# Last layer of a four-layer graph network: the features become the stationary operand for three of four quarters

## Chip, cores, metric

One core of a Trainium2 chip runs one program. The metric is the device time of one execution in microseconds (us), the median of several runs. Everything is fp32 except a uint8 copy of the adjacency's pattern.

## The reference, cut to what matters

x has 4096 rows of 128 features, adj is 4096 x 4096. Four layers follow each other, each on h = relu(layernorm(x)) and added to x. The change touches the last one alone:

```
def _L3_gnn_ref(X, H):
    msg = jnp.matmul(H.T, X)
    inv_deg = 1.0 / H.sum(axis=0)
    inv_deg = jnp.where(jnp.isinf(inv_deg), 0.0, inv_deg)
    return msg * inv_deg[:, None]
h = jnp.maximum(_layernorm(x, axis=-1), 0.0)
x = x + _L3_gnn_ref(h, adj)
```

Row i of the result is the sum over j of adj[j, i] * h[j, :], divided by the sum of column i of adj.

## The kernel before

T = 32 tiles of P = 128 rows cover the 4096 rows; the output is made in Q = 4 quarters of S = 8 tiles (QC = 1024 rows). The code numbers the passes over adj by h = 0 to 4 (the second layer has two heads, h = 1 and 2), and layer 3 and layer 4 stand below for the passes h = 3 and h = 4, the last being `_L3_gnn_ref`.

In a quarter q the loop `run(h, q, hooks)` (line 387) goes over the 32 source tiles k. `products` (line 310) then does 8 products, one for each output tile s: the stationary operand is a 128x128 block of the adjacency tile, the moving operand is G[:, ., k, :], 129 columns wide (DW): 128 features and a column of ones, whose product gives the column sum of adj. Results go to acc, three banks of PSUM (NB = 3) with 3, 3 and 2 output tiles of 129 columns. In layer 4 the adjacency tiles come straight from memory: SyncE (`stream`, called by `layer3`, lines 234 and 250) brings 128x1024 tiles, 512 KB each, into DEEP = 8 slots of stream3, which lies over the memory of the mask. A slot is filled again when TensorE has finished with it (semaphore deep_used).

At the end of a quarter ScalarE's `take` (line 681) copies the three banks to U, each as soon as it is summed (acc_summed), and tells acc_taken; TensorE waits for a bank's acc_taken only when it starts that bank anew. VectorE's `post3` (line 1191) makes the divisors out of the 129th column, multiplies and adds X, and ScalarE issues the store (`store`, line 802). The last quarter is done bank by bank (line 1209 on) and stored by SyncE. U is [P, 8 * 129]; flat is a view of its first 1024 columns.

The order on each engine is the order of the code. `hooks` is a table from k to small groups of work put into the stream behind step k. `quarters` (line 214) is a loop of the hardware, so that its body stands once in the program; a quarter with a fixed number stands apart. Beside acc, PSUM holds turn (two banks, used for transposes) and mix, of whose third bank `one` is the first 128 columns. ring has 5 slots of 1024 columns: slot 0 is R, 1 to 3 hold the weighted adjacency tiles E of layers 1 to 3, slot 4 holds small constants.

Around the start of layer 4: SyncE issues its first 8 tiles once all E of layer 3 are made (line 289). VectorE runs the rest of layer 3's last quarter (`post2`, and `feed` with the statistics for the layer norm), and ScalarE writes the last 8 tiles of G, which TensorE waits for at k = 24 of quarter 0 (f_norm).

Of the kernel before, what the change touches and what calls it, by code (L numbers as in the profile page):

```python
# [30 lines left out]
P = 128  # L31
ALU = mybir.AluOpType
# [32 lines left out]
def graph_layers(nc, x, adj, adj_t, diag, alpha, w0_t, bias0, ff0, ff0_t, ff1_t, attn, g1, b1, g2, b2,  # L65
                 w2, w2_t, a2, out, inputs1):
    N, D = x.shape
    T = N // P
# [14 lines left out]
    with ExitStack() as ctx:  # L83
        def sb(name, shape, dt=F32):
            return ctx.enter_context(nc.sbuf_tensor(name, shape, dt))

        def sem(name):
            return ctx.enter_context(nc.semaphore(name))
# [17 lines left out]
        dev = sb("dev", [P, S])  # L106
        scale = sb("scale", [P, S])
        shift = sb("shift", [P, S])
        cols = sb("cols", [P, 32])
        rq = sb("rq", [P, S])  # L110
        inv = sb("inv", [P, S])
        zero = sb("zero", [P, S])
# [23 lines left out]
        hmean = cols[:, 24:25]  # L136
        seen = cols[:, 25:26]
        first_top, fall, vfix, wfix = [cols[:, i:i + 1] for i in range(26, 30)]
        warm = {ACT.Sqrt: cols[:, 30:31], ACT.Exp: cols[:, 31:32]}

        acc = ctx.enter_context(nc.psum_tensor("acc", [P, NB, BANK], F32))
# [50 lines left out]
        own_made = sem("own_made")  # L192
        inv_ready, divided = sem("inv_ready"), sem("divided")
        post_done = sem("post_done")

        n_var, n_dev, n_scale, n_norm = sem("n_var"), sem("n_dev"), sem("n_scale"), sem("n_norm")
        n_turned, n_wide, ff_done, exp_made, half_made = sem("n_turned"), sem("n_wide"), sem("ff_done"), sem("exp_made"), sem("half_made")
# [4 lines left out]
        def fixed(v):  # L202
            return isinstance(v, int)
# [6 lines left out]

        def width(b):
            return min(3, S - 3 * b)

        def quarters(eng, first, last, body, steps=None, per_turn=0):

            with eng.Fori(first, last + 1) as q:
                if steps:
                    steps.enter(q - first if first else q, per_turn)
                body(q)
            if steps:  # L220
                steps.leave(last + 1 - first)

        def wait(eng, signal, count):

            if not fixed(count) or count > 0:
                eng.wait_ge(signal, count)

        @block.sync
        def _(sp):  # L230
            def load_x(t, n, loaded):
                sp.dma_start(X[:, t:t + n, :], x[t * P:(t + n) * P, :].rearrange("(s p) d -> p s d", p=P)).then_inc(loaded, 16)  # L232

            def stream(src, slots, loaded, used, h, q, some=range(T)):

                L = len(loaded)
                for k in some:
                    if k >= L:
                        sp.wait_ge(used, q * (T - 1) + k - L + 1)
                    elif not fixed(q) and k == L - 1:  # L240
                        sp.wait_ge(acc_summed[NB - 1], q + h * Q)
                    elif not fixed(q):
                        sp.wait_ge(used, q * (T - 1) + k - L + 2)
                    sp.dma_start(slots(k % L), span(src[k * P:(k + 1) * P, :], q * QC, QC))\  # L244
                        .then_inc(loaded[k % L], 16)

            def layer0(q, some=range(T)):
                stream(adj_t, lambda s: ring[:, s, :], slot_loaded, slot_used, 0, q, some)

            def layer3(q):  # L250
                stream(adj, lambda s: stream3[:, s, :], deep_loaded, deep_used, 4, q)

            load_x(0, S // 2, x_first)
            load_x(S // 2, S // 2, x_loaded[0])
            sp.dma_start(w0T, w0_t).then_inc(w0_loaded, 16)
            layer0(0, range(2))
            load_x(S, S, x_loaded[1])
            layer0(0, range(2, STREAM))
            load_x(2 * S, S, x_loaded[2])
            load_x(3 * S, S, x_loaded[3])  # L260
            loads = [(bias0_b, bias0.partition_broadcast(P)), (alphac, alpha.partition_broadcast(P)),
                     (w2raw, w2_t), (attnc[:, 0:4], attn), (attnc[:, 4:6], a2), (dsub[:, :], diag),
                     (proj1[:, 0:D], ff0_t[0]), (ff0T1, ff0_t[1])]
            loads += [(ff0raw[h], ff0[h]) for h in range(HEADS)]
            loads += [(c, v.rearrange("(c o) -> c o", o=1)) for c, v in ((g1c, g1), (b1c, b1), (g2c, g2), (b2c, b2))]
            loads += [(ff1T[:, :, :], ff1_t.rearrange("h c o -> c h o"))]
            assert len(loads) == WEIGHTS
            for dst, src in loads:
                sp.dma_start(dst, src).then_inc(weights_loaded, 16)  # L269
            layer0(0, range(STREAM, T))  # L270
            quarters(sp, 1, Q - 1, layer0)

            sp.wait_ge(qv_summed, 1)
            sp.dma_start(proj2[:, 0:D], w2).then_inc(w2_loaded, 16)

            sp.wait_ge(saved, 16 * Q)

            def bring_back(q):  # L280
                if fixed(q):
                    sp.wait_ge(post_done, 2 * Q)
                else:
                    sp.wait_ge(f_turned, q + 3 * Q)
                sp.dma_start(V[:, :, :].rearrange("p s d -> p (s d)"), span(inputs1, q * QC, QC)).then_inc(back, 16)
            bring_back(0)
            quarters(sp, 1, Q - 1, bring_back)

            sp.wait_ge(e_made, 3 * Q * T)
            layer3(0)  # L290
            quarters(sp, 1, Q - 1, layer3)
            for b in range(NB):
                sp.wait_ge(last_made, b + 1)
                some = slice(3 * b, 3 * b + width(b))
                sp.dma_start(out.rearrange("(t p) d -> p t d", p=P)[:, (Q - 1) * S:, :][:, some, :], V[:, some, :])\
                    .then_inc(stored, 16)
            sp.wait_ge(stored, 16 * (Q - 1 + NB))
# [11 lines left out]
        def _(pe):  # L309
            def products(n, k, lhs, g, done, fix):  # L310

                for s in range(S):
                    b = s // 3
                    if fix and k == EARLY and s % 3 == 0:
                        pe.wait_ge(acc_scaled, fix * NB - NB + b + 1)
                    if k == 0 and s % 3 == 0:
                        wait(pe, acc_taken, n * NB - NB + b + 1 if not (fixed(n) and n == 0) else 0)
                    mm = pe.matmul(acc[:, b, (s % 3) * DW:(s % 3) * DW + DW], lhs[:, s * P:(s + 1) * P], g,  # L318
                                   start=(k == 0 and s % 3 == 0), stop=(k == T - 1), skip_group_check=True)
                    if k == T - 1 and (s % 3 == 2 or s == S - 1):  # L320
                        mm.then_inc(acc_summed[b], 1)
                    elif s == S - 1:
                        mm.then_inc(done, 1)
                    elif fix and k == EARLY - 1 and s % 3 == 2:
                        mm.then_inc(acc_paused[b], 1)
# [166 lines left out]
            run(3, Q - 1, {})  # L492

            run(4, 0, {})
            quarters(pe, 1, Q - 1, lambda q: run(4, q, {}))

        @block.scalar
        def _(act):  # L500
# [299 lines left out]

            def store(q):
                take(q + 4 * Q)
                act.wait_ge(post_done, q + 4 * Q + 1)
                act.dma_start(span(out.rearrange("(t p) d -> p t d", p=P), q * S, S), V[:, :, :]).then_inc(stored, 16)
            quarters(act, 0, Q - 2, store)
            take(5 * Q - 1)

        @block.vector  # L810
        def _(dve):
# [180 lines left out]
                return dict(zip(ks, steps))  # L992

            for i in range(2):
                dve.memset(G[:, i, :, D], 1.0)
            st.mark(dve.memset(hmean, 0.0))
# [186 lines left out]
                run(3, q, at([1, 6, 8, 11, 14, 17], post2(q - 1) + feed(4, q - 1 + 4 * Q, q - 1)))  # L1184
            quarters(dve, 1, Q - 2, stage3, st, STAGE3)
            stage3(Q - 1)
            for step in post2(Q - 1) + feed(4, 5 * Q - 1, Q - 1):
                step()

            def post3(q):
                dve.wait_ge(acc_taken, (q + 4 * Q + 1) * NB)
                st.then(dve.tensor_scalar(zero[:, :], Ud, 0.0, None, ALU.is_equal))  # L1193
                st.then(dve.tensor_tensor(inv[:, :], Ud, zero[:, :], ALU.add))
                st.then(dve.reciprocal(inv[:, :], inv[:, :]))
                st.then(dve.tensor_scalar(zero[:, :], zero[:, :], -1.0, 1.0, ALU.mult, ALU.add))
                st.then(dve.tensor_tensor(inv[:, :], inv[:, :], zero[:, :], ALU.mult))
                if not fixed(q):
                    dve.wait_ge(stored, q * 16)
                for s in range(S):  # L1200
                    ins = dve.scalar_tensor_tensor(V[:, s, :], U3[:, s, 0:D], inv[:, s:s + 1], blocks(X, q, 1, s)[:, 0, :],
                                                   ALU.mult, ALU.add)
                ins.then_inc(post_done, 1)
            post3(0)
            quarters(dve, 1, Q - 2, post3, st, 5)

            dve.wait_ge(stored, (Q - 1) * 16)
            for b in range(NB):
                dve.wait_ge(acc_taken, (5 * Q - 1) * NB + b + 1)
                some = slice(3 * b, 3 * b + width(b))  # L1210
                z, i = zero[:, some], inv[:, some]
                st.then(dve.tensor_scalar(z, U3[:, some, D], 0.0, None, ALU.is_equal))  # L1212
# [37 lines left out]
```

## Time and profile before

| | us |
|---|---|
| median of 3 runs | 1274.88 |
| lowest, highest | 1274.65, 1276.23 |
| span of the profiled execution | 1272.8 |
| TensorE products busy in it | 1246.4 (98%) |
| TensorE weight loads busy | 1235.7 (97%) |
| VectorE busy | 754.2 (59%) |
| ScalarE busy | 349.8 (27%) |

The span runs from the first to the last instruction on the core, in one profiled execution; the metric also contains what lies around it, so that the median stands 2.1 us above this span. In the views PE is TensorE's products, PEld its weight loads, DVE VectorE, ACT ScalarE, SPq and ACTq the queues that issue transfers.
### The profile page before, as it was taken

How to read it: one execution, taken by the hardware profiler on the slowest of the kernel's cores; microseconds unless marked ns; L12 is line 12 of the kernel's file. 1: busy time of each engine (PE TensorE's matmuls, PEld its weight loads, DVE VectorE, ACT ScalarE, POOL GpSimd, SP SyncE). 2: the span in 40 equal slices, each digit the busy share in tenths (PEclk: the TensorE clock that was granted, in tenths of full speed). 3: DMA queues.
4: the chain of work that ended last, by engine and by line, in shares of the span. 5: the costliest groups of instructions: out<-in, count | busy, mean ns of one | idle time of the engine just before them, and what ended most of it. 6: DMA issues, size and time to landing. Idle time of an engine off the chain costs nothing.

```text
span 1272.8 us, 26806 instructions
## 1 busy us (share of the span) xinstructions
PE 1246.4 (98%) x10979; PEld 1235.7 (97%) x10979; DVE 754.2 (59%) x1348; ACT 349.8 (27%) x872; POOL 0.7 (0%) x6
## 2 busy tenths in 40 slices
PE   7999999999999999999999999999999999999997
PEld 6999999999999999999999999999999999999997
DVE  4336363659686868687979797878697850000001
ACT  3313121324835353432333233443232120000000
POOL 0000000000000000000000000000000000000000
PEclk9999999999999999999999999999999999999999
DMA  7678787850000000000000000000000058889884
GB/s 221 228 250 265 253 262 257 270 197 2 18 2 18 0 16 0 16 1 18 2 18 0 16 1 18 2 1 1 1 0 1 1 196 317 313 293 309 294 310 148
DMA packets 49037, 144.40 MB, mean 113 GB/s; under 512 B 5696, under 2 KB 15168, under 8 KB 48960
## 3 DMA queue, kind: packets, MB, share of 16 engines
q1 hardware_dynamic: 45264, 139.63, 32.7%
q10 hardware_dynamic: 3696, 3.67, 0.8%
q8 instruction: 57, 0.93, 0.3%
q14 instruction: 20, 0.16, 0.0%
HBM read 139.09 MB, written 4.19 MB: 113 GB/s over the span
## 4 chain that ended last, share of the span: by engine, by line
PE 83%; DMA 7%; DVE 6%; SPq 2%; ACT 1%; issue 1%; DVEq 0%; ACTq 0%
PE acc L318 77%; DMA ring<-in_adj_t 7%; PE mix L352 2%; DVE ring L982 2%; PE turn L333 1%; PE mix L369 1%; DVE mask L1017 1%; PE turn L329 1%; SPq L269 1%; ACT V L511 1%; SPq L232 0%; DVE stats L829 0%; DVE stats L825 0%; SPq L244 0%; DVE mask L1063 0%
## 5 line engine op out<-in xcount | busy, mean ns | idle before, releaser
L318 PE MATMUL acc<-G,ring 128*128 128x129 f32 x8192 | 942.1, 276 | 13.8 <-DVE mask L1017 9.4
L318 PEld LDWEIGHTS acc<-G,ring 128*128 128x128 f32 x8192 | 927.2, 192 | 23.0 <-DVE mask L1017 6.9
L982 DVE SCALAR_TENSOR_TENSOR ring<-ring,score,mask 128x1024 f32<-128x1024 f32 x384 | 483.7, 1281 | 136.4 <-PE acc L318 130.7
L318 PE MATMUL acc<-G,mask 128*128 128x129 f32 x2048 | 229.0, 275 | 0.0
L318 PEld LDWEIGHTS acc<-G,mask 128*128 128x128 f32 x2048 | 228.8, 192 | 0.1
L1017 DVE TENSOR_SCALAR mask<-ring 128x1024 uint8<-128x1024 f32 (+1 forms) x128 | 88.7, 693 | 133.9 <-DMA ring<-in_adj_t 133.4
L687 ACT COPY U<-acc 128x387 f32<-128x387 f32 (+1 forms) x60 | 25.3, 458 | 269.9 <-PE acc L318 268.7
L1193 DVE TENSOR_SCALAR zero<-U 128x8 f32<-128x8 f32 x3 | 0.5, 172 | 153.5 <-ACT U L687 153.5
L523 ACT ACTIVATE dev<-var 128x8 f32<-128x8 f32 x28 | 5.9, 211 | 246.6 <-DVE var L838 246.6
L652 ACT COPY ring<-turn 128x512 f32<-128x512 f32 x14 | 8.2, 586 | 121.7 <-DVE ring L982 114.0
L503 ACT COPY cols<-ident 128x1 f32<-128x1 f32 x44 | 8.6, 196 | 103.3 <-DVE shift L848 41.0
L511 ACT ACTIVATE V<-X,shift,scale 128x128 f32<-128x128 f32 (+1 forms) x92 | 36.8, 484 | 0.0
L533 ACT ACTIVATE U<-turn,cols 128x512 f32<-128x512 f32 x32 | 23.2, 774 | 45.2 <-PE turn L333 45.2
L507 ACT ACT_TABLE_LOAD x26 | 33.4, 1283 | 1.2 <-PEq L1229 0.8
L352 PE MATMUL mix<-ring,U 128*128 128x128 f32 (+2 forms) x256 | 32.5, 282 | 1.2 <-ACT U L535 1.2
L352 PEld LDWEIGHTS mix<-ring,U 128*128 128x128 f32 x256 | 31.2, 198 | 1.4 <-ACT U L535 1.4
L1212 DVE TENSOR_SCALAR zero<-U 128x3 f32<-128x3 f32 (+1 forms) x3 | 0.5, 163 | 52.8 <-ACT U L687 52.8
L511 ACT ACTIVATE V<-U,shift,scale 128x128 f32<-128x128 f32 x64 | 25.6, 484 | 10.2 <-DVE shift L848 10.2
L587 ACT COPY G<-mix 128x384 f32<-128x384 f32 (+3 forms) x36 | 14.8, 461 | 47.6 <-PE mix L352 47.6
L333 PE MATMUL turn<-ident,V 128*128 128x128 f32 x192 | 25.0, 273 | 2.5 <-ACT V L511 2.5
L511 ACT ACTIVATE V<-X,norms 128x128 f32<-128x128 f32 (+1 forms) x64 | 25.6, 489 | 0.1
L333 PEld LDWEIGHTS turn<-ident,V 128*128 128x128 f32 x192 | 21.7, 141 | 2.9 <-issue 1.7
(129 smaller groups left out, 449.4 us busy)
## 6 DMA issues: line engine op xcount, KB each, us to landing
ring<-in_adj_t SPq DMA_DIRECT2D x128, 512.0 KB, 4.6
mask<-in_adj SPq DMA_DIRECT2D x128, 512.0 KB, 4.6
inputs<-V ACTq DMA_DIRECT2D x4, 512.0 KB, 2.6
V<-inputs SPq DMA_DIRECT2D x4, 512.0 KB, 4.0
X<-in_x SPq DMA_DIRECT2D x3, 512.0 KB, 9.5
out_x<-V ACTq DMA_DIRECT2D x3, 512.0 KB, 8.5
X<-in_x SPq DMA_DIRECT2D x2, 256.0 KB, 3.3
out_x<-V SPq DMA_DIRECT2D x2, 192.0 KB, 2.1
```

The costliest lines, as they stand in the source:

```text
L269: sp.dma_start(dst, src).then_inc(weights_loaded, 16)
L318: mm = pe.matmul(acc[:, b, (s % 3) * DW:(s % 3) * DW + DW], lhs[:, s * P:(s + 1) * P], g, start=(k == 0 and s % 3 == 0), stop=(k == T - 1) ...
L329: return pe.transpose(dst, col.broadcast_to([P, P]), ident[:, :])
L333: mm = pe.transpose(turn[:, s * P:(s + 1) * P], V[:, s, :], ident[:, :])
L352: mm = pe.matmul(mix[:, s // 3, (s % 3) * PW:(s % 3) * PW + wide], U[:, s * P:(s + 1) * P], weights, start=True, stop=True, skip_group_che ...
L507: act.activation(warm[func], ident[:, 0:1], func)
L511: ins = act.activation(dst(s), src(s), func, bias=add(s), scale=mul(s))
L533: ins = act.activation(dst, src, ACT.Identity, bias=bias_, scale=scale_)
L587: ins = act.copy(blocks(G[:, h % 2, :, :], q, c, 3 * b)[:, :, 0:D], got[:, :, 0:D])
L687: act.copy(U[:, b * 3 * DW:b * 3 * DW + w], acc[:, b, 0:w]).then_inc(acc_taken, 1)
L982: dve.scalar_tensor_tensor(E[k % EB], R, rank[h][:, k:k + 1], span(mask, q * QC + k * N, QC), ALU.max, ALU.mult).then_inc(e_made, 1)
L1017: dve.tensor_scalar(span(mask, q * QC + k * N, QC), ring[:, k % STREAM, :], 0.0, None, ALU.is_gt).then_inc(mask_made, 1)
```

## The change

Quarters 0 to 2 of layer 4 are computed the other way round. The stationary operand is the 128x128 block of features G[:, 0, k, 0:D], the moving operand the adjacency tile in two halves of 512 columns. Two banks of acc gather the transposed result, features by output rows. So a step of k has 2 products of 512 columns in place of 8 of 129 (`by_features`).

The column sums are no longer a by-product. VectorE adds the tiles (`column_sums`): even k into ring slot 0 or 2, odd k into slot 1 or 3 (by the quarter's parity), the first two as copies, and then the two partial sums, 33 instructions a quarter. TensorE sums what is left over the partitions with 8 products of one moving column of ones (`columns`, line 517 of the new kernel), behind k = 4 of the next quarter. A slot of stream3 is free only when both TensorE (deep_used, wide_summed) and VectorE (col_added) have used it.

At the end of a quarter ScalarE copies the two banks to flat, 512 columns each (wide_taken). TensorE turns them back with 8 transposes behind k = 2 of the next quarter (`turn_back`), and VectorE makes divisors and output from turn and one behind its sums 6 and 7. The last quarter is computed as before, but its first product waits for both copies of quarter 2, and it carries the transposes and column products of quarter 2. Layer 3's post-processing, which VectorE did without anything between, now stands between the sums of quarter 0. The loops over the quarters of layer 4 are written out.

```diff
@@ SyncE
             def layer3(q):
-                stream(adj, lambda s: stream3[:, s, :], deep_loaded, deep_used, 4, q)
+                for k in range(T):
+                    n = q * T + k - DEEP
+                    if n >= 0:
+                        if k % T == DEEP - 1 and q:
+                            sp.wait_ge(wide_summed, 2 * q)
+                        else:
+                            sp.wait_ge(deep_used, n - n // T + 1)
+                        if n < (Q - 1) * T:
+                            sp.wait_ge(col_added, n + n // T + 1)
+                    sp.dma_start(stream3[:, k % DEEP, :], adj[k * P:(k + 1) * P, q * QC:(q + 1) * QC])\
+                        .then_inc(deep_loaded[k % DEEP], 16)
@@ TensorE
-            run(4, 0, {})
-            quarters(pe, 1, Q - 1, lambda q: run(4, q, {}))
+            def columns(q):
+
+                pe.wait_ge(col_added, (q + 1) * (T + 1))
+                wait(pe, post_done, q and 4 * Q + q)
+                for s in range(S):
+                    mm = pe.matmul(one[:, s:s + 1], column_part(q, 0)[:, s * P:(s + 1) * P], ones,
+                                   start=True, stop=True, skip_group_check=True)
+                mm.then_inc(col_summed, 1)
+
+            def turn_back(q):
+
+                pe.wait_ge(wide_taken, 2 * (q + 1))
+                for s in range(S):
+                    mm = pe.transpose(turn[:, s * P:(s + 1) * P], flat[:, s * P:(s + 1) * P], ident[:, :])
+                mm.then_inc(back_turned, 1)
+
+            def by_features(q, hooks):
+
+                for k in range(T):
+                    pe.wait_ge(deep_loaded[k % DEEP], (q * (T // DEEP) + k // DEEP + 1) * 16)
+                    if q == 0 and k % S == 0:
+                        pe.wait_ge(f_norm, 4 * Q + k // S + 1)
+                    for c in range(2):
+                        if k == 0 and q == 0:
+                            pe.wait_ge(acc_taken, (4 * Q - 1) * NB + c + 1)
+                        elif k == 0:
+                            pe.wait_ge(wide_taken, 2 * (q - 1) + c + 1)
+                        mm = pe.matmul(acc[:, c, :], G[:, 0, k, 0:D], stream3[:, k % DEEP, c * BANK:(c + 1) * BANK],
+                                       start=(k == 0), stop=(k == T - 1), skip_group_check=True)
+                        if k == T - 1:
+                            mm.then_inc(wide_summed, 1)
+                        elif c == 1:
+                            mm.then_inc(deep_used, 1)
+                    if k in hooks:
+                        hooks[k]()
+
+            def behind(q):
+                return {2: lambda: turn_back(q), 4: lambda: columns(q)}
+            by_features(0, {})
+            for q in range(1, Q - 1):
+                by_features(q, behind(q - 1))
+            pe.wait_ge(wide_taken, 2 * (Q - 1))
+            run(4, Q - 1, behind(Q - 2))
@@ ScalarE
             def store(q):
-                take(q + 4 * Q)
+                if q:
+                    act.wait_ge(back_turned, q)
+                for c in range(2):
+                    act.wait_ge(wide_summed, 2 * q + c + 1)
+                    act.copy(flat[:, c * BANK:(c + 1) * BANK], acc[:, c, :]).then_inc(wide_taken, 1)
@@ VectorE
-            for step in post2(Q - 1) + feed(4, 5 * Q - 1, Q - 1):
+
+            def column_sums(q, hooks):
+
+                for k in range(T):
+                    dve.wait_ge(deep_loaded[k % DEEP], (q * (T // DEEP) + k // DEEP + 1) * 16)
+                    if q == 0 and k == 0:
+                        dve.wait_ge(e_made, 3 * Q * T)
+                    if q == 0 and k == 1:
+                        dve.wait_ge(acc_summed[NB - 1], 4 * Q)
+                    part, tile = column_part(q, k), stream3[:, k % DEEP, :]
+                    if k < 2:
+                        if q >= 2:
+                            dve.wait_ge(col_summed, q - 1)
+                        dve.tensor_copy(part, tile).then_inc(col_added, 1)
+                    else:
+                        dve.wait_ge(col_added, q * (T + 1) + k - 1)
+                        dve.tensor_tensor(part, part, tile, ALU.add).then_inc(col_added, 1)
+                    if k in hooks:
+                        hooks[k]()
+                dve.wait_ge(col_added, q * (T + 1) + T)
+                dve.tensor_tensor(column_part(q, 0), column_part(q, 0), column_part(q, 1), ALU.add).then_inc(col_added, 1)
...
+            column_sums(0, at([1, 5, 7, 8, 9, 11], post2(Q - 1) + feed(4, 5 * Q - 1, Q - 1)))
+            for q in range(1, Q - 1):
+                column_sums(q, at([6, 7], post3(q - 1)))
+            for step in post3(Q - 2):
                 step()
```

The order of TensorE's instructions in the whole of layer 4, before: quarter 0, then the loop's body (one quarter, stood for once), in rows of like instructions (a product counts once here).

```order
L318 MATMUL acc<-G,mask 128x129 x256
L216 UNCONDITIONAL_BRANCH
L216 ISA
L226 ISA
L318 MATMUL acc<-G,mask 128x129 x3
L226 REGISTER_ALU
L318 MATMUL acc<-G,mask 128x129 x61
```

And in the new kernel, from the end of layer 3 to the end of the program (L335 is the narrow product, L539 the wide one, L525 the transposes, L517 the column products; acc, turn and mix are PSUM, G the features, mask the memory of the streamed tiles):

```order
L335 MATMUL acc<-G,ring 128x129 x256
L539 MATMUL acc<-mask,G 128x512 x70
L525 MATMUL turn<-ident,U 128x128 x8
L539 MATMUL acc<-mask,G 128x512 x4
L517 MATMUL mix<-cols,ring 128x1 x8
L539 MATMUL acc<-mask,G 128x512 x60
L525 MATMUL turn<-ident,U 128x128 x8
L539 MATMUL acc<-mask,G 128x512 x4
L517 MATMUL mix<-cols,ring 128x1 x8
L539 MATMUL acc<-mask,G 128x512 x54
L335 MATMUL acc<-G,mask 128x129 x24
L525 MATMUL turn<-ident,U 128x128 x8
```

Three times 256 narrow products have become 70 + 4 + 60 + 4 + 54 = 192 wide ones, with two of the three pairs of inserted groups between them; the third pair stands in the narrow last quarter.

VectorE at the start of layer 4, before: the last tiles E of layer 3 (L982), its post-processing (L1168 to L1178) and the statistics (L825 on).

```order
L982 SCALAR_TENSOR_TENSOR ring<-ring,score,mask 128x1024 x14
L1168 TENSOR_SCALAR zero<-U 128x8
L1169 TENSOR_TENSOR inv<-U,zero 128x8
L1170 RECIPROCAL inv<-inv 128x8
L1175 TENSOR_TENSOR U<-U,V 128x8x128
L1178 SCALAR_TENSOR_TENSOR X<-U,X 128x1024
L825 BN_STATS stats<-X 128x6 x4
```

The same place in the new kernel: the sums (L1269, the copies L1266) with layer 3's post-processing (L1234 to L1244) and statistics (L890 on) between them.

```order
L1266 COPY ring<-mask 128x1024 x2
L1234 TENSOR_SCALAR zero<-U 128x8
L1235 TENSOR_TENSOR inv<-U,zero 128x8
L1236 RECIPROCAL inv<-inv 128x8
L1269 TENSOR_TENSOR ring<-ring,mask 128x1024 x4
L1241 TENSOR_TENSOR U<-U,V 128x8x128
L1269 TENSOR_TENSOR ring<-ring,mask 128x1024 x2
L1244 SCALAR_TENSOR_TENSOR X<-U,X 128x1024
L1269 TENSOR_TENSOR ring<-ring,mask 128x1024
L890 BN_STATS stats<-X 128x6 x4
L1269 TENSOR_TENSOR ring<-ring,mask 128x1024
L894 BN_STATS stats<-X 128x6 x4
```

So 2 copies and 8 sums of 1024 columns now stand ahead of the second half of the statistics, where before these steps followed each other directly.

## Rows read from the trace of the kernel before

**Rows 1.** The page: busy tenths in 40 slices of the span, and granted clock.

```profile
PE   7999999999999999999999999999999999999997
DVE  4336363659686868687979797878697850000001
PEclk9999999999999999999999999999999999999999
```

**Rows 2.** Chain that ended last, its last links: start, us, what.

```profile
916.33 57.22 PE acc L318 x512
974.42 290.30 PE acc L318 x2598
```

**Rows 3.** Groups of layer 4, 1036.9 to 1265.6 us: busy us, mean ns | idle before.

```profile
L318 PE MATMUL acc<-G,mask 128*128 128x129 f32 x2048 | 229.0, 275 | 0.0
L318 PEld LDWEIGHTS acc<-G,mask 128*128 128x128 f32 x2048 | 228.8, 192 | 0.1
```

**Rows 4.** Busy time by windows: layer 4, and one quarter of layer 3.

```profile
core 0: us, PE busy (x) PEld busy (x) DVE busy (x) ACT busy (x) POOL busy (x), PEclk, DMA share, GB/s
1036.86:1265.82 228.96, 228.96 (x2049) 228.77 (x2048) 15.43 (x64) 13.79 (x41) 0.00 (x0) 1.00 0.84 296
916.33:973.38 57.05, 57.05 (x512) 57.05 (x512) 45.01 (x54) 13.84 (x36) 0.00 (x0) 1.00 0.00 0
```

**Rows 5.** Timeline around 83 us (start us, us, engine): products of two moving columns.

```profile
83.05 0.75 PEld L428 LDWEIGHTS mix<-cols,ring 128*128 128x128 f32 x6
83.16 0.73 PE L428 MATMUL mix<-cols,ring 128*128 128x2 f32 x6
...
83.72 0.64 PEld L318 LDWEIGHTS acc<-G,ring 128*128 128x128 f32 x5
```

**Rows 6.** Timeline of TensorE, 200 and 337 to 347 us: 132 columns, transposes, 128 columns.

```profile
200.40 1.97 PE L352 MATMUL mix<-ring,U 128*128 128x132 f32 x16
202.20 9.10 PE L318 MATMUL acc<-G,ring 128*128 128x129 f32 x80
...
337.52 1.04 PE L333 MATMUL turn<-ident,V 128*128 128x128 f32 x8
338.39 3.74 PE L318 MATMUL acc<-G,ring 128*128 128x129 f32 x32
...
344.63 1.95 PE L352 MATMUL mix<-ring,U 128*128 128x128 f32 x16
346.42 27.21 PE L318 MATMUL acc<-G,ring 128*128 128x129 f32 x240
```

**Rows 7.** Line 652, a copy of 512 columns from PSUM: ns min/median/max.

```profile
L652 ACT COPY ring<-turn x14: 586/586/587, 278.4 to 975.0; 128x512 f32<-128x512 f32 x14
```

**Rows 8.** Timeline 688 to 693 us: transposes, ScalarE's copies, the products behind them.

```profile
687.80 0.93 PE L333 MATMUL turn<-ident,V 128*128 128x128 f32 x7
...
688.82 1.45 ACT L533 ACTIVATE U<-turn,cols 128x512 f32<-128x512 f32 x2 [1.91 <-PE turn L333]
...
690.39 1.86 PEld L369 LDWEIGHTS mix<-ff1T,U 128*128 128x128 f32 x16
690.40 2.05 PE L369 MATMUL mix<-ff1T,U 128*128 128x128 f32 x16
```

**Rows 9.** Line 1175, an addition of 1024 columns on VectorE: ns min/median/max.

```profile
L1175 DVE TENSOR_TENSOR U<-U,V x4: 1218/1219/1226, 872.1 to 1043.0; 128x1024 f32<-128x1024 f32 x4
```

**Rows 10.** Timeline 1043 to 1060 us: scale and the last 8 tiles of G.

```profile
1048.47 0.20 DVE L844 RECIPROCAL scale<-dev 128x8 f32<-128x8 f32 x1 [0.40 <-ACT dev L523]
...
1049.00 3.19 ACT L511 ACTIVATE G<-X,shift,scale 128x128 f32<-128x128 f32 x8
```

**Rows 11.** Tile in_adj: from issue to landing of the 128 loads of layer 4.

```profile
DMA to landing us min/median/max: 3.9/4.6/10.6
```

**Rows 12.** Transfers, 1033 to 1045 us in 40 slices: GB/s.

```profile
GB/s 0 0 0 177 218 328 246 328 382 437 396 410 382 246 287 369 382 382 369 382 341 314 314 423 423 410 396 369 423 396 410 423 437 423 410 396 437 410 410 396
```

**Rows 13.** Timeline 1030 to 1045 us: the start of layer 4.

```profile
1032.95 11.69 SPq L244 DMA_DIRECT2D mask<-in_adj  x12
1035.93 1.44 ACT L687 COPY U<-acc 128x387 f32<-128x387 f32 x3 [24.39 <-PE acc L318]
...
1036.86 8.31 PE L318 MATMUL acc<-G,mask 128*128 128x129 f32 x72
```

**Rows 14.** Timeline 1215 to 1273 us: the last copies, VectorE's last instruction.

```profile
1264.80 1.44 ACT L687 COPY U<-acc 128x387 f32<-128x387 f32 x3 [55.74 <-PE acc L318]
...
1269.98 0.62 DVE L1218 SCALAR_TENSOR_TENSOR V<-U,inv,X 128x128 f32<-128x128 f32 x2
```

## What the change will do to the time: the prediction

> **What bounds the kernel now.** The page first: TensorE is busy in every tenth of the span and at the granted clock of 2.4 GHz, while VectorE has nothing to do in the last fifth [rows 1]. The last entry of the chain of waits is one unbroken run of line 318, from layer 3 to the last product of layer 4 [rows 2]. So in the stretch that is changed nothing but TensorE sets the time, and the groups of that stretch say it again: 229.0 us of products with 0.0 us idle, over 1024 logical products that the chip runs as 2048 instructions, since an fp32 product is two [rows 3]. By the window over layer 4 a step of k (8 products, 16 instructions) takes 228.96 us less 0.17 for the drain of the last one, over 128 steps: 1.7875 us, or **111.7 ns an instruction**.
>
> What are these 111.7 ns? Weight loads are as full as the products, 228.77 us [rows 4]. Six instructions with only 2 moving columns have their weight loads from 83.05 to 83.72, 112 ns each [rows 5]: with 64 times fewer columns the pace is the same. The 128-column products run 16 in 1.79 us, 111.9 ns [rows 6]. So the narrow stream goes by its weight load, one 128-column fp32 load in 111.7 ns. What the columns cost by themselves shows where the load doesn't decide: the transposes, one instruction each, take 0.87 us for 8, 108.8 ns, and at 132 columns 16 instructions take 1.80 us, 112.5 ns [rows 6]. At 2.4 GHz these are 261 and 270 cycles, two cycles for each column and 5 to 6 besides. A narrow one of 129 would then need 258 + 6 cycles, 110 ns, just under its load.
>
> **Wide products, the gain.** A 512-column instruction should take 1024 + 6 cycles, 429.2 ns, and its load of 112 ns hides behind the one before. A step of k becomes 2 products, 4 instructions: 1.717 us instead of 1.7875, 0.0707 less. Three quarters have 96 steps: **-6.8 us**. The bounds: with no fixed part, 1.7067 us and -7.8; with a fixed part that grows with the columns (108.8 / 128 or 112.5 / 132 a column), 435 to 436.4 ns, 1.740 to 1.746 us and -4.6 to -4.0. I take the constant one, since 128 and 132 columns leave the same 5 to 6 cycles.
>
> **Column sums on TensorE, a cost.** Line 517 of the new kernel has 8 one-column products a quarter, 16 instructions. Their price is the weight load, 111.7 ns by the 2-column row [rows 5]: 1.79 us a quarter. A wide product before them hides the first load, and the next wide one waits for its own, so 16 stay. Three times: **+5.4 us**. All three lie in TensorE's stream, behind k = 4 of the next quarter, and nothing hides them.
>
> **Turning back, a cost.** 8 transposes a quarter at 108.8 ns [rows 6], 0.87 us, three times: **+2.6 us**. The rows show each lasting 273 ns, but the next one starts after 109. The Trainium skill, page TensorE: Matmul & The Clock Gate, Part 4, puts a transpose within a kernel at about 275 ns. At 275 ns each, 24 of them would be 6.6 us and the sum 4.0 us higher; I go by the start-to-start time, as the trace has 8 in 0.87 us at 2.4 GHz.
>
> **Hand-overs between quarters, a cost.** Before, a bank is copied out while the other two are still summed, and TensorE never waits. Now there are two banks and each copy moves 512 columns from PSUM, 0.586 us [rows 7]. The trace shows such a hand-over around 688 us: the last transpose ends at 687.80 + 0.93 = 688.73, ScalarE starts at 688.82, 0.09 later, and ends at 688.82 + 1.45 = 690.27, the first weight load starts 0.12 later and the group of 16 lasts 2.05 instead of 1.95 us, since the first load isn't hidden [rows 8]. A wide instruction ends some 0.165 us after the next could start (275 less 110 ns, [rows 3]). So from the point where the next product could start: 0.165 + 0.09 + 0.586 + 0.12 + 0.10 = 1.06 us until a product that needs the copy starts. Into quarters 1 and 2 the other bank's products (0.858 us) lie between: 0.1 to 0.2 us lost, twice; its own copy is then done in time. Into quarter 3 the kernel waits for both copies ahead of the first narrow product: the whole 1.06. Together **+1.3 us** (0.9 to 1.5).
>
> **What is hidden.** VectorE adds each 128x1024 tile once more: 33 instructions a quarter at 1.22 us [rows 9], two of them copies that I bound by the same 1.22 and by half of it, 40 us in a quarter of 55 us. In quarter 0 the last steps of layer 3's post-processing stand between the sums (about 6 us, from line 1168 on): the scale for the last 8 tiles of G then comes at 1038 + 12 sums x 1.22 + 6 = 1059 instead of 1048.5, and ScalarE needs 3.2 us more [rows 10]; TensorE wants them at k = 24, 1036.86 + 24 x 1.717 = 1078. In quarters 1 and 2 VectorE stops behind sum 6 until TensorE has done k = 4 and the column products, about 11.3 us in. Queued behind that wait are the sums 7 to 31, and on them SyncE's loads (its queue now waits for the sum too) from k = 15 on. TensorE wants that tile at 1.717 x 15 + 2.7 = 28.4 us; the slot's sum is done by about 16, and a tile lands about 5 us after its issue [rows 11]: over 7 us to spare. **Transfers:** a 512 KB tile every 1.717 us is 305 GB/s; the queue moved 437 GB/s in its best slices while it filled [rows 12], against 296 over the layer [rows 4]. Layer 4 starts on the landing of tile 0, as now [rows 11, 13]; tile 2 may be late by hundredths. The steps of the last tiles and the stores are as before, so what follows the last product stays at 7 us [rows 14].
>
> **Sum.** -6.8 + 5.4 + 2.6 + 1.3 = +2.5 us. The profiled execution has a span of 1272.8 us, 2.1 below the median of 1274.88 us; its span would be 1275.3, and the time **1277.4 us**, 0.2% more. A measurement of this kernel tells about 0.2%, 2.55 us, from no change, so the forecast lies at that bound, a hair inside.
>
> **Rivals.**
> - The fixed part grows with the columns (a 512-column stream is held up in itself, as by reads of the moving tile while DMA writes and VectorE reads the same memory). It decides as soon as an instruction takes over 430 ns: slower. Price 2.2 to 2.8 us: 1279.6 to 1280.2. For it: no row has more than 132 columns. Against: with VectorE busy for 45.01 of 57.05 us beside it, TensorE kept 57.22 us for 512, the same 111.8 ns [rows 2, 4]. Chance 0.13.
> - VectorE becomes the bound. A sum then takes over 1.717 us a tile, since it reads a tile that TensorE streams. Each 0.1 us above that costs 9.6 us over 96 tiles. Against: adds of this size took 1.22 us. Chance 0.05, 1281 to 1290.
> - The column products' weight loads hide behind the wide ones altogether. The cost of 5.4 us falls to near nothing: 1272.0. Against: six loads in a row came at 112 ns each though the products between them had 2 columns [rows 5]. Chance 0.02, faster.
> - Wide products overlap each other. The same page of the Trainium skill, section Back-to-back issue gap, has a sustained 81 ns at 128 columns and 131 ns at 512. As a mechanism of this kernel: were an instruction of 512 columns under 223 ns (twice a narrow one), a step would be under 0.9 us, tiles at 437 GB/s (1.20 us) and sums at 1.22 us would set the pace, 96 x (1.7875 - 1.22) = 54 us would go and 9.3 be added: about 1230. Against: four more columns cost 3.7 ns, all of their two cycles each [rows 6]. Chance 0.01.
>
> **Chances.** The forecast's case has 0.75, with its own range of 1276.1 (no fixed part, cheap hand-overs) to 1278.0; it is cut by the bound into 0.40 same and 0.35 slower. With 0.04 left for what I don't see, split between same and slower: faster 0.03, same 0.42, slower 0.55. The range takes in the first rival and the scatter of the runs, 1275.7 to 1280.5.
>
> **What the new profile would show.** Wide instructions 429 ns apart, so 55 us for a quarter of 128 of them (a step over 1.73 us: the first rival). Between them, 16 instructions of one column in 1.8 us and 8 transposes in 0.87. TensorE idle only at the ends of quarters, 1.0 us in front of the narrow last quarter, released by ScalarE's copy. No wait of TensorE for DMA or for VectorE past the first tiles; VectorE busy some 70% of quarters 0 to 2. A last quarter of 57.2 us and 2.7 for its two inserted groups. I am wrong if TensorE waits inside a quarter, or if the wide step isn't within 0.01 us of 1.717.

## The result, and the profile after

The changed kernel takes 1277.64 us (median of 17 runs, 1273.97 to 1280.51), the kernel before 1274.65 (17 runs, 1271.46 to 1276.5): a ratio of 1.0024, 95% interval 1.0016 to 1.0033. It is slower by a quarter of a per cent, where 0.20% was forecast. The profiled execution has a span of 1277.4 us against 1272.8, 4.6 more, and the first reading is where these 4.6 us lie. The windows of the two profiles, changed kernel first, then before (us, busy us of each engine with instructions, clock, transfers' share, GB/s):

```profile
0.10:285.51 285.41, 267.70 (x2269) 261.28 (x2269) 140.60 (x386) 71.64 (x194) 0.70 (x6) 0.99 0.77 246
285.51:1038.75 753.24, 749.73 (x6665) 745.99 (x6663) 593.85 (x880) 263.53 (x638) 0.00 (x0) 1.00 0.02 8
1038.86:1270.37 231.51, 230.83 (x970) 137.83 (x968) 129.09 (x163) 13.45 (x38) 0.00 (x0) 1.00 0.84 293
```

```profile
0.10:283.44 283.34, 267.61 (x2268) 260.98 (x2269) 140.39 (x385) 71.57 (x194) 0.70 (x6) 0.99 0.77 248
283.44:1036.68 753.24, 749.62 (x6664) 745.91 (x6663) 594.02 (x880) 263.88 (x638) 0.00 (x0) 1.00 0.02 8
```

Layer 0 is 2.1 us longer though nothing in it changed; the passes of layers 1 to 3 are equal to 0.01 us in these two profiles; layer 4 went from 228.96 [rows 4] to 231.51 us, **+2.55**, and what follows it is 7.0 us in both. In layer 0 the work waits for transfers: VectorE's masks wait for them, and TensorE waited 12.4 us for the masks, against 9.4 in the profile before. In the ten profiles of this case, all with the same code for layer 0, it ended anywhere from 281.1 to 288.8 us, and layers 1 to 3 took from 753.15 to 753.74 us. So single executions differ by microseconds in layer 0 and by half of one in layers 1 to 3, and the change is read in layer 4, where stretches of the same instructions repeat to 0.1 us.

A part of layer 0's scatter is TensorE's clock. The same stretch of layer 0, changed kernel first, then before:

```profile
101.50:104.90 3.40, 3.08 (x14) 3.08 (x15) 3.27 (x8) 0.00 (x0) 0.00 (x0) 0.50 0.40 155
101.50:104.90 3.40, 3.35 (x28) 3.00 (x27) 3.21 (x8) 0.00 (x0) 0.00 (x0) 1.00 0.77 257
```

Behind an idle time of 2.38 us the granted clock was 1.2 GHz for these 3.4 us, and 14 instructions came where 28 did before, some 1.5 us of work at 111.7 ns each. Of the ten profiles three have such a stretch near 105 us, and their layer 0 is the longest (285.5, 287.2 and 288.8 us; the others end by 284.9).

The page of the changed kernel, in 40 slices (the rows that answer to [rows 1]; PEld is weight loads):

```profile
PE   7998999999999999999999999999999999999997
PEld 6998999999999999999999999999999974444497
DVE  4445363659686868687979797878687878677401
PEclk9999999999999999999999999999999999999999
```

TensorE is as full as before, at the same clock, but in the wide quarters its weight loads are busy for four tenths only, and VectorE is busy for 86%, 71% and 64% of quarters 0, 1 and 2. The weight loads were relieved and TensorE's own stream was not: its timeline in layer 4 (start us, us, engine, line, out<-in) has every term of the sum.

```profile
1038.86 60.49 PE L539 MATMUL acc<-mask,G 128*128 128x512 f32 x140
1099.18 1.04 PE L525 MATMUL turn<-ident,U 128*128 128x128 f32 x8
1100.06 3.60 PE L539 MATMUL acc<-mask,G 128*128 128x512 f32 x8
1103.49 1.84 PE L517 MATMUL mix<-cols,ring 128*128 128x1 f32 x16
1105.19 51.95 PE L539 MATMUL acc<-mask,G 128*128 128x512 f32 x120
1156.98 1.04 PE L525 MATMUL turn<-ident,U 128*128 128x128 f32 x8
1157.86 3.60 PE L539 MATMUL acc<-mask,G 128*128 128x512 f32 x8
1161.29 1.84 PE L517 MATMUL mix<-cols,ring 128*128 128x1 f32 x16
1162.99 46.60 PE L539 MATMUL acc<-mask,G 128*128 128x512 f32 x108
1210.26 5.63 PE L335 MATMUL acc<-G,mask 128*128 128x129 f32 x48 [0.67 <-ACT U L865]
```

Take differences of starts: 8 wide instructions from 1100.06 to 1103.49, 3.43 us, 429 ns each; 8 transposes in 0.88; 16 column instructions in 1.70, and the wide one behind them begins its columns 0.08 late, as its weight load came last, so 1.78 in all. Into quarter 3 there is an idle time of 0.67 us that ScalarE's copy ended. The 140 in the first row have the hand-over into quarter 1 among them: 60.32 us less 140 x 0.4292 leaves 0.23, which is 0.04 at the layer's start and 0.2 at the hand-over.

What TensorE waited for in layer 4, beside its own stream (us in total, times, longest): its products once, its weight loads for ScalarE's copies and for tiles that hadn't landed.

```profile
PE acc L335 <- ACT U L865: 0.7, 1, 0.7
PEld acc L335 <- ACT U L865: 1.5, 1, 1.5
PEld acc L539 <- ACT U L865: 0.9, 2, 0.4
PEld acc L539 <- DMA mask<-in_adj: 0.5, 2, 0.2
PEld acc L539 <- ACT U L745: 0.2, 1, 0.2
```

### The profile page after: what moved, and what is told of

It reads as the page before. It is cut to its first block, busy times and chain, and to the rows that moved or that the text cites. A ratio compares the mean times of both kernels' runs of the same rounds, so it can differ in the third digit from the quotient of the medians.

```text
span 1277.4 us, 24572 instructions
## 1 busy us (share of the span) xinstructions
PE 1248.4 (98%) x9899; PEld 1145.2 (90%) x9899; DVE 868.0 (68%) x1448; ACT 349.1 (27%) x869; POOL 0.7 (0%) x6
## 4 chain that ended last, share of the span: by engine, by line
PE 83%; DMA 7%; DVE 6%; SPq 2%; ACT 1%; issue 1%; DVEq 0%; ACTq 0%
PE acc L335 64%; PE acc L539 13%; DMA ring<-in_adj_t 7%; PE mix L369 2%; DVE ring L1047 2%; PE turn L350 2%; PE mix L386 1%; DVE mask L1083 1%; SPq L285 1%; PE turn L346 1%; SPq L238 1%; ACT V L569 0%; PE mix L517 0%; DVE stats L894 0%; DVE stats L890 0%
## 5 line engine op out<-in xcount | busy, mean ns | idle before, releaser
L335 PE MATMUL acc<-G,ring 128*128 128x129 f32 x8192 | 943.0, 276 | 16.2 <-DVE mask L1083 12.4
L335 PEld LDWEIGHTS acc<-G,ring 128*128 128x128 f32 x8192 | 928.5, 192 | 25.2 <-DVE mask L1083 8.4
L539 PE MATMUL acc<-mask,G 128*128 128x512 f32 x384 | 166.2, 593 | 0.0
L539 PEld LDWEIGHTS acc<-mask,G 128*128 128x128 f32 x384 | 72.5, 190 | 90.0 <-issue 88.3
L1269 DVE TENSOR_TENSOR ring<-ring,mask 128x1024 f32<-128x1024 f32 x90 | 107.3, 1222 | 22.4 <-DMA mask<-in_adj 21.5
L335 PEld LDWEIGHTS acc<-G,mask 128*128 128x128 f32 x512 | 57.4, 192 | 1.5 <-ACT U L865 1.5
L335 PE MATMUL acc<-G,mask 128*128 128x129 f32 x512 | 57.9, 275 | 0.7 <-ACT U L865 0.7
L745 ACT COPY U<-acc 128x387 f32<-128x387 f32 (+1 forms) x51 | 21.5, 459 | 120.5 <-PE acc L335 119.2
L865 ACT COPY U<-acc 128x512 f32<-128x512 f32 x6 | 3.5, 585 | 144.4 <-PE acc L539 144.4
```

Source lines behind the costliest of these rows:

```text
L539: mm = pe.matmul(acc[:, c, :], G[:, 0, k, 0:D], stream3[:, k % DEEP, c * BANK:(c + 1) * BANK], start=(k == 0), stop=(k == T - 1), skip_gro ...
L745: act.copy(U[:, b * 3 * DW:b * 3 * DW + w], acc[:, b, 0:w]).then_inc(acc_taken, 1)
L1269: dve.tensor_tensor(part, part, tile, ALU.add).then_inc(col_added, 1)
```

## Experiments

All were read in layer 4, from the start of TensorE's first instruction of the layer to that of its last: 228.7 us before, 231.2 in the changed kernel. Experiments 1 to 6 are one execution each, and their whole times are not used, since layer 0 is in them: experiment 4 took 1281.17 us with a layer 4 no longer than the changed kernel's.

**1. Is the narrow stream set by its weight loads?**

```diff
-                    mm = pe.matmul(acc[:, b, (s % 3) * DW:(s % 3) * DW + DW], lhs[:, s * P:(s + 1) * P], g,
+                    mm = pe.matmul(acc[:, b, (s % 3) * DW:(s % 3) * DW + w], lhs[:, s * P:(s + 1) * P], g[:, 0:w],
```

with w = 64 in layer 4 of the kernel before, 129 elsewhere.

> The kernel before, with 64 moving columns in place of 129 in every product of layer 4 (half of the features and the column sums are left out of the last layer). Theory, the narrow stream goes by its weight load: layer 4 takes 228.7 us between its first and last product, as before, 111.7 ns an instruction. Rival, the columns decide: an instruction takes 56 ns and the layer goes by its transfers, 150 us or so, the whole some 75 us less.

Measured 228.6 us. The window over layer 4 (columns as above):

```profile
1037.06:1265.92 228.86, 228.86 (x2050) 228.72 (x2048) 15.43 (x64) 13.84 (x41) 0.00 (x0) 1.00 0.85 297
```

Half the columns, the same 111.7 ns an instruction. The columns don't decide, with half of them to spare: in the narrow form 65 of 129 columns are free, and so was the 129th with its column sum. For the load, and against a fixed pace of any instruction, speak the transposes, which follow each other after 109 ns: their loads are shorter. From the changed kernel's layer 4:

```profile
L335 PEld LDWEIGHTS acc<-G,mask 128*128 128x128 f32 x512 | 57.4, 192 | 1.5 <-ACT U L865 1.5
L525 PEld LDWEIGHTS turn<-ident,U 128*128 128x128 f32 x24 | 2.8, 142 | 1.1 <-issue 1.1
```

A load lasts 192 ns for a product and 142 for a transpose. No experiment made a product's load shorter, so this last step is argued, not shown by a run of its own.

**2. What does an instruction cost besides its columns?** The changed kernel, each product of 512 columns as two of 256:

```diff
-                        mm = pe.matmul(acc[:, c, :], G[:, 0, k, 0:D], stream3[:, k % DEEP, c * BANK:(c + 1) * BANK],
-                                       start=(k == 0), stop=(k == T - 1), skip_group_check=True)
+                        for i in range(2):
+                            lo = i * (BANK // 2)
+                            mm = pe.matmul(acc[:, c, lo:lo + BANK // 2], G[:, 0, k, 0:D],
+                                           stream3[:, k % DEEP, c * BANK + lo:c * BANK + lo + BANK // 2],
+                                           start=(k == 0 and i == 0), stop=(k == T - 1), skip_group_check=True)
```

> The changed kernel, each product of 512 columns made as two of 256. Theory, two cycles a column and a constant 2.5 ns for each instruction: 215.8 ns each, a step of k 1.727 us, layer 4 0.96 us longer than the 231.2 us between first and last product that the changed kernel has. Rival, the part above two cycles grows with the columns: the layer keeps its 231.2 us. Weight loads are twice as many and stay hidden by both.

Measured 232.1 us, 0.9 longer. In its timeline:

```profile
1100.14 3.62 PE L541 MATMUL acc<-mask,G 128*128 128x256 f32 x16
1103.59 1.84 PE L517 MATMUL mix<-cols,ring 128*128 128x1 f32 x16
```

16 in 3.45 us. Over all undisturbed starts of the layer the mean distance is 215.8 ns; 512 columns give 429.2 and the transposes' 128 gave 109.2. The first narrow product of quarter 3 comes 172.32 us after the layer's start, where the changed kernel has 171.40: 0.92 us for 384 instructions more, 2.4 ns each. The distances at 128, 256 and 512 columns are all two cycles a column at 2.4 GHz and 2.5 ns besides, so the part that doesn't grow with the columns is constant over a factor of four. The first rival of the prediction, a fixed part that grows with the columns, is refuted.

**3. What do the column products cost?** The changed kernel with `for s in range(1)` in `columns` in place of `range(S)`.

> The changed kernel with one of eight column products a quarter (seven eighths of the column sums are left out, so the divisors are wrong). Theory, each costs two weight loads of 111.7 ns with nothing to hide them: 42 fewer instructions, 4.7 us less in layer 4, 226.5 us. Rival, what costs is the entry into the group, whatever its length: under 2 us less.

Measured 226.5 us, 4.7 less. Two instructions are left of each 16:

```profile
1098.27 3.60 PE L539 MATMUL acc<-mask,G 128*128 128x512 f32 x8
1101.71 0.28 PE L517 MATMUL mix<-cols,ring 128*128 128x1 f32 x2
1101.85 51.95 PE L539 MATMUL acc<-mask,G 128*128 128x512 f32 x120
```

42 instructions fewer and 4.70 us: 112 ns each. A product of one column pays the whole load of 128, and a wide product ahead hides one load, not the row of them.

**4. Do VectorE's sums cost anything?** The changed kernel without the additions (only the two copies a quarter stay, and SyncE waits for VectorE at these alone):

```diff
...
-                        dve.wait_ge(col_added, q * (T + 1) + k - 1)
-                        dve.tensor_tensor(part, part, tile, ALU.add).then_inc(col_added, 1)
+                        dve.wait_ge(col_added, 2 * q + 1)
...
-                dve.wait_ge(col_added, q * (T + 1) + T)
-                dve.tensor_tensor(column_part(q, 0), column_part(q, 0), column_part(q, 1), ALU.add).then_inc(col_added, 1)
```

> The changed kernel without the additions on VectorE (the column sums hold one tile of 32; the copies and the post-processing stay). Theory, the sums are hidden and don't slow TensorE's reads: layer 4 keeps 231.2 us within 0.2. Rival, VectorE's reads of the tile that TensorE streams hold it up: wide instructions come closer than 429 ns and the layer is over 0.5 us shorter.

Measured 231.2 us, and 8 wide instructions between two groups in 3.44 us, where 3.43 stood with the sums, though VectorE is busy for 19.3 us of the layer instead of 129.1. That VectorE reads the tiles that TensorE streams doesn't slow TensorE here. The transfers stayed in both.

**5. And if they took longer than TensorE's step?** Every addition made twice, 2.4 us a tile against 1.717.

> The changed kernel with every addition on VectorE made twice (the column sums come out wrong), 2.44 us a tile. Theory, VectorE hides as long as it stays under 1.717 us a tile and sets the pace above: 63 additions and 2 copies a quarter, 79 us, and its other steps 6 and 3 us, layer 4 about 310 us, TensorE waiting for the loads that VectorE's sums let go. Rival, the slack of 8 slots takes most of it up: under 280 us.

Measured 287.7 us: longer by 56.5, between the two expectations. TensorE now waits as forecast (us in total, times, longest):

```profile
PEld acc L539 <- DMA mask<-in_adj: 71.2, 56, 3.4
PE acc L539 <- DMA mask<-in_adj: 26.5, 49, 2.5
PEld mix L517 <- DVE ring L1274: 8.2, 3, 3.1
```

The mechanism is that of the theory and its size was wrong. The copies are 0.69 us each, not 1.22, and there are 61 additions a quarter, not 63. VectorE ends its last sum of quarter 2 at 1273.0 us, 236 after the layer's start. But the 8 slots let TensorE run ahead of it: its narrow quarter starts at 1259.65, 222.6 after the layer's start, 13.4 us before VectorE is done, and takes 65.1 us with its own waits: 287.7. The slots take up a debt once, not per quarter. A second cost came with the waits: behind four of them, 2.0 to 2.5 us long, the granted clock fell from 2.4 to 1.2 GHz, for 17 us in all. One of these stretches, 1275.9 to 1279.3 us, lies in the narrow quarter, whose last 432 instructions took 50.1 us in place of 48.5. In the changed kernel the clock is granted in full throughout layer 4. Where between 1.22 and 2.4 us a tile the waits begin, no run shows.

**6. Are the hand-overs avoidable?** Quarters 0 and 2 sum into two banks of mix, quarter 1 into acc:

```diff
+        def wide_bank(q, c):
+            return acc[:, c, :] if q % 2 else mix[:, c, :]
...
-            pe.wait_ge(wide_taken, 2 * (Q - 1))
+            pe.wait_ge(wide_taken, 2 * (Q - 2))
```

> The changed kernel with the quarters' wide sums alternately in two other PSUM banks (quarters 0 and 2) and in the old ones (quarter 1), so that no product waits for a copy of the quarter just ended. Theory, the hand-overs cost what the changed kernel's trace shows, 0.20 twice and 0.94 us: layer 4 from 231.2 to 229.9 us, wide instructions 429 ns apart across the quarters' ends. Rival, the wait is drain of the wide products and stays: over 230.8 us.

Measured 229.95 us, 1.28 less, and the narrow quarter follows its predecessor without an idle time:

```profile
1158.78 46.60 PE L540 MATMUL mix<-mask,G 128*128 128x512 f32 x108
1205.22 5.52 PE L338 MATMUL acc<-G,mask 128*128 128x129 f32 x48
```

So the hand-overs were waits for copies of a bank that was needed again, not the wide products' drain.

**7. Column sums off TensorE.** VectorE turns the summed tile in blocks of 32x32 and adds each block's 32 columns; one product with a stationary matrix of ones where row and column agree modulo 32 adds the four partition groups; a small masked sum on VectorE picks the block of each partition.

```diff
-                for s in range(S):
-                    mm = pe.matmul(one[:, s:s + 1], column_part(q, 0)[:, s * P:(s + 1) * P], ones,
-                                   start=True, stop=True, skip_group_check=True)
-                mm.then_inc(col_summed, 1)
+                pe.matmul(one[:, 0:32], every32, folded, start=True, stop=True,
+                          skip_group_check=True).then_inc(col_summed, 1)
...
+                st.then(dve.transpose(column_part(q, 1), column_part(q, 0)))
+                if q:
+                    dve.wait_ge(col_summed, q)
+                dve.reduce_sum(folded, column_part(q, 1).rearrange("p (b j) -> p b j", j=32), AX_X).then_inc(col_folded, 1)
```

> The changed kernel with the last step of the column sums taken from TensorE: VectorE turns the summed tile in blocks of 32x32, adds each block's 32 columns, and a single product of 32 columns adds the four partition groups. Theory, the eight column products cost 16 weight loads a quarter and the single one 2: layer 4 from 231.2 to 226.5 us, the time 4.7 us under the changed kernel's 1277.6 and 1.7 us under the kernel before's 1274.65, a ratio of 0.9985. Rival, VectorE's two further instructions of 1024 elements come late for TensorE: a wait in front of the product, over 228 us.

Layer 4 measured 226.6 us, as the theory has it. The time, 1273.5 us in 12 runs against 1273.85 in 17 of the kernel before on the same chip, is a ratio of 0.9996 with an interval of 0.998 to 1.0011: the 1.7 us expected against before lie inside it, and no more can be said. This is also the run whose layer 0 took longest in the profile, 288.8 us.

**8. All quarters wide.** Folded sums, banks in turn, and quarter 3 wide as well. The divisors are made from the folded sums before the last product, and the end runs in two halves:

```diff
-            run(4, Q - 1, behind(Q - 2))
+            by_features(Q - 1, behind(Q - 2) | {30: lambda: columns(Q - 1)})
+            for c in range(2):
+                pe.wait_ge(wide_taken, 2 * (Q - 1) + c + 1)
+                for s in range(4 * c, 4 * c + 4):
+                    mm = pe.transpose(turn[:, s * P:(s + 1) * P], flat[:, s * P:(s + 1) * P], ident[:, :])
+                mm.then_inc(back_turned, 1)
...
```

> As with the folded sums and the banks in turn, and quarter 3 wide too, its divisors made ahead of its end and the last results turned back, divided and stored in two halves. Theory: 128 steps of 1.717 us are 219.8, four single column products 0.9, three groups of transposes 2.6, the last copy and transposes 1.5: 224.7 us from first to last TensorE instruction of the layer in place of 228.7 before, and 3.8 us behind the last one in place of 7.3, since no divisor is left to make. Together 7.5 us under the kernel before, 1267.2 us, a ratio of 0.994. Rival, what follows the last product grows by what the copy and the transposes add, as TensorE has nothing to do beside them: no better than 1271 us.

Measured 1268.09 us (6 runs) against 1273.85: a ratio of **0.995, interval 0.9932 to 0.9969**. It is 5.8 us faster than the kernel before, where 7.5 were expected (a ratio of 0.994, inside the interval). The changed kernel wasn't timed beside it; against the kernel before that one stands at 1.0024. Layer 4 is 224.6 us from first to last instruction, and 4.5 us follow where 7.3 did. The end of its timeline:

```profile
1258.70 0.30 PE L524 MATMUL mix<-score,ff1T 128*128 128x32 f32 x2
1258.84 1.96 PE L543 MATMUL acc<-mask,G 128*128 128x512 f32 x4
...
1260.68 1.46 PE L561 MATMUL turn<-ident,U 128*128 128x128 f32 x8
...
1261.47 2.16 DVE L1325 SCALAR_TENSOR_TENSOR V<-turn,inv,X 128x128 f32<-128x128 f32 x8 [0.96 <-PE turn L561]
1262.62 1.42 SPq L319 DMA_DIRECT2D out_x<-V  x2
```

Copy, transposes and results overlap by halves, and VectorE's last work is 2.2 us of results instead of three banks of five small steps, 0.2 us each, and results. Two things lengthen what follows, which came 0.7 us longer than the 3.8 expected; how much each has of it isn't shown. VectorE still works on the first half when the second is turned (1262.14; its second half starts at 1262.51). And the last store is one of four tiles, which is over 2.7 us after VectorE's end, where before the store of two took 2.2. By the two profiles layer 4 and what follows take 229.1 us against 236.0, 6.9 less; the medians, with the scatter of layer 0 in them, differ by 5.8.

## Why the prediction was right

The sum was -6.8 + 5.4 + 2.6 + 1.3 = +2.5 us; layer 4 measured +2.55.

- **What bounds.** The narrow stream doesn't go by its columns: experiment 1 showed it in the layer itself, over 2048 instructions of 64 columns. For the weight load as what sets its pace speak the transposes, which have shorter loads and come 109 ns apart.
- **Wide products, -6.8.** 429.2 ns an instruction was forecast. The layer's timeline has 429, and 96 steps of 1.717 give -6.8. The constant part was taken from columns of 128 and 132; experiment 2 placed a third point at 256.
- **Column products, +5.4.** Measured 3 x 1.78 = 5.3, and by experiment 3 it is 112 ns for each instruction.
- **Turning back, +2.6.** 0.87 to 0.88 us for 8. The 275 ns of the Trainium skill (TensorE: Matmul & The Clock Gate, Part 4) is the duration of one, 273 in the rows here, and not its cost in a stream: 109 ns from start to start, with the clock granted in full.
- **Hand-overs, +1.3.** Measured 0.20 twice and 0.94 into quarter 3 (0.84 before its first instruction, 0.10 for the first weight load), 1.34 in all; experiment 6 recovered 1.28. The forecast had 1.06 for the last. ScalarE starts 0.04 us after a product there, not 0.09, and TensorE's first load 0.05 us after the copy, not 0.12.
- **What is hidden.** VectorE's additions took 1.22 us as forecast and the copies 0.69; experiment 4 shows the additions free. The scale for the last tiles of G came at 1058.64 in the new profile, whose layer starts 2 us later, where I had 1059; TensorE did not wait for it. No wait of TensorE for VectorE appears, and for transfers 0.5 us of weight loads at the layer's start, 0.04 of it on the stream.
- **The rivals.** Growing fixed part: refuted by experiment 2. VectorE as the bound: real at 2.4 us a tile, as experiment 5 shows, but not at 1.22. Loads all hidden behind the wide products: refuted by experiment 3. Wide products that overlap, by the Trainium skill's figures for 128 and 512 columns on the same page (section Back-to-back issue gap): no run here shows it, as 128, 256 and 512 columns came 109, 215.8 and 429 ns apart.

The time came out 0.24% above before where the sum gives 0.20%. The difference of 0.5 us is inside the interval, which spans 2.2 us. Layer 0 scatters by microseconds and layers 1 to 3 by 0.6 us from one execution to the next, so it needs no cause in layer 4. That 1277.4 lies only 0.24 us below the median of 1277.64 has some luck in it: the forecast started from a median of 3 runs that stands 0.23 us above that of 17. The ends of the forecast's own range aren't quite those of its terms: they give 1276.0 where 1276.1 stands, and 1277.6, with 1.5 us for the hand-overs, where 1278.0 stands.

## What to carry to other kernels

Before widening the moving operand, ask which of the two streams, weight loads or columns, sets the pace, and by how much: here they were 111.7 ns measured and 110 worked out, so that with the 129th column and the fixed part of 12 instructions a step all that widening could gain was 4% of the stretch. A by-product that rode along free (a 129th column) has its full price once the form changes, and a short product with 128-column weights pays two whole weight loads for it; see first whether an idle engine can fold the data, so that one product is left (experiment 7: 4.6 us less in layer 4). When one stretch of a kernel scatters by microseconds, read the change in its own stretch.

## What the runs showed of the hardware that was not expected

- An fp32 instruction with 64 moving columns keeps the pace of one with 129, 111.7 ns (experiment 1). Where the load doesn't decide, in the transposes of 128 columns and the products of 256 and 512, one takes 2 cycles a column at 2.4 GHz and 2.5 ns: 109.2, 215.8 and 429.2 ns.
- VectorE copies 128x1024 fp32 in 0.69 us, where adding takes 1.22; turning it in 32x32 blocks takes 1.25, and adding 32 columns at a time 1.22.
- A bank that is copied out and needed again costs 0.2 us at a change of quarter although 0.86 us of the other bank's products lie between, and 0.94 us where none do: a copy of 0.59 us is 0.4 to 0.5 longer from product to product.
- TensorE's granted clock fell from 2.4 to 1.2 GHz behind idle times of 2.0 to 2.7 us, in layer 0 of three profiles and four times in layer 4 of experiment 5, and instructions came at half the rate while it lasted. In layer 4 of the changed kernel, where its longest idle time is 0.67 us, it stayed at 2.4 GHz.
